# Output bias added by an accumulating DMA, half of the last sums on POOL, waits and router steps rearranged in a cross-attention and routed-FFN kernel

## The reference

```
def layernorm(x): return (x - mean(x)) / sqrt(var(x) + 1e-5)      # over the 256 features

q = layernorm(x) @ Wq + bq                # x, ctx: (128, 128, 256)
k, v = split(ctx @ Wkv + bkv)             # 16 heads of 16 each
scores = q @ k.T / 4
attn = softmax(scores, axis=2)            # over the QUERIES, not the keys
x1 = x + (attn @ v) @ Wo + bo

s = layernorm(x1) @ w_router              # one score for each token
top = the 96 of 128 tokens with the highest s, in each batch
h = layernorm(x1)
out = x1 + (gelu_tanh(h @ w_block) where in top, h elsewhere)
```

## Time and profile before

| | |
|---|---|
| median of 3 runs | 938.55 us (938.32 to 939.42) |
| the profiled execution | 938.16 us, of which the span from first to last instruction is 936.2 us |
| mean granted TensorE clock | 0.988 of 2.4 GHz |
| PE / PEld busy | 896.5 us (96%) / 758.3 us (81%) |
| DVE busy | 880.6 us (94%) |
| ACT busy | 875.5 us (94%) |
| POOL busy | 798.4 us (85%) |
| DMA | 70.84 MB, 25.6% of 16 engines on SP's queue |

### The profile page before, as it was taken

How to read it: one execution, slowest core, us unless ns; L and a number is a source line. 1 busy time by engine, 2 the same in 40 slices (tenths; PEclk the granted TensorE clock), 3 DMA queues, 4 the chain that set the end, 5 groups by cost and what they waited for, 6 DMA issues and landing times. The chain is left out here.

```text
span 936.2 us, 32893 instructions
## 1 busy us (share of the span) xinstructions
PE 896.5 (96%) x10296; PEld 758.3 (81%) x10296; DVE 880.6 (94%) x2318; ACT 875.5 (94%) x4499; POOL 798.4 (85%) x1488
## 2 busy tenths in 40 slices
PE   6899999999999999999999999999999999999972
PEld 5688888888888888888888888888888888888861
DVE  4898999999999999999999999999999999999877
ACT  2899999999999999999999999999999999999983
POOL 4367789999999999999999989999999999998865
PEclk8999999999999999999999999999999999999997
DMA  6222222232232232232223123223223223211102
GB/s 186 74 52 59 64 69 56 82 92 55 85 91 59 83 89 72 72 87 73 73 85 92 55 85 92 57 82 92 59 83 91 58 85 88 79 54 54 47 25 91
DMA packets 71244, 70.84 MB, mean 76 GB/s; under 512 B 12192, under 2 KB 62880, under 8 KB 71072
## 3 DMA queue, kind: packets, MB, share of 16 engines
q1 hardware_dynamic: 71072, 68.73, 25.6%
HBM read 35.13 MB, written 16.78 MB: 55 GB/s over the span
## 5 line engine op out<-in xcount | busy, mean ns | idle before, releaser
L532 ACT ACTIVATE e_sb<-ps_s,neg_max 128x128 f32<-128x128 f32 x2048 | 717.2, 411 | 8.3 <-DVE neg_max L644 8.2
L532 ACT ACTIVATION_READ_ACCUMULATOR e_sb<-ps_s,neg_max 128x1 f32 x2048 | 515.4, 252 | 0.0
L644 DVE TENSOR_REDUCE neg_max<-ps_s 128x4 f32<-128x512 f32 x512 | 330.5, 667 | 35.7 <-PE ps_s L324 35.2
L324 PE MATMUL ps_s<-q_eo,k_sb 32*128 32x256 f32 x2048 | 147.6, 401 | 9.7 <-DMA q_eo<-q_raw 3.6
L377 PE MATMUL ps_a<-e_sb,v_pad 128*32 128x128 f32 x4096 | 138.4, 276 | 2.1 <-POOL v_pad L969 0.7
L294 PE MATMUL ps_a<-w_o_sb,o_sb 128*128 128x256 f32 x512 | 135.7, 387 | 2.3 <-DVE v_sb L736 2.0
L969 POOL TENSOR_TENSOR v_pad<-v_sb,recip 128x256 f32<-128x256 f32 x128 | 79.4, 620 | 67.8 <-DVE recip L688 62.5
L294 PE MATMUL ps_t<-w_z_sb,xt_sb 128*128 128x258 f32 x512 | 132.7, 381 | 1.4 <-DVE z_sb L747 1.4
L324 PEld LDWEIGHTS ps_s<-q_eo,k_sb 32*128 32x128 f32 x2048 | 95.6, 185 | 39.0 <-issue 33.4
L377 PEld LDWEIGHTS ps_a<-e_sb,v_pad 128*32 128x32 f32 x4096 | 104.1, 109 | 24.0 <-issue 21.7
L959 POOL TENSOR_TENSOR x_sb<-x_sb,bo_sb 128x256 f32<-128x256 f32 x128 | 119.0, 931 | 0.2
(11 more groups left out here) (92 smaller groups left out, 2199.2 us busy)
## 6 DMA issues: line engine op xcount, KB each, us to landing
x_sb<-in_x SPq DMA_DIRECT2D x64, 256.0 KB, 2.9
c_sb<-in_ctx SPq DMA_DIRECT2D x64, 256.0 KB, 3.1
q_eo<-q_raw SPq DMA_DIRECT2D x512, 32.0 KB, 2.0
out<-z_sb SPq DMA_DIRECT2D x64, 256.0 KB, 2.4
...
```

What stands on the lines that cost most here:

```text
L324: mm = nc.tensor.matmul(ps_s[:, bank(b, j), c, :, :], k_sb[rows, r2, c, h * T:(h + 1) * T], q_eo[rows, r2, :, c, h, :], start=True, stop=True)
L532: last = nc.scalar.activation(e_sb[:, b % 4, j, c, par, :], ps_s[:, bank(b, j), c, par, :], ACT.Exp, bias=neg_max[:, b % 4, h:h + 1], accu ...
L644: nc.vector.tensor_reduce(neg_max[:, b % 4, :].rearrange("p (c j q) -> p j c q", c=C, j=J)[:, j, :, :], ps_s[:, bank(b, j), :, :, :], AX.X ...
```

## The change

Four things are changed together.

1. The output bias is no longer added to x by a POOL instruction for each batch. POOL issues one DMA for four batches that adds bo_sb to x_sb while it writes (`inputs_and_bias`); the residual waits for its landing (`xb_in`). 32 DMAs take the place of 128 instructions.
2. For the odd batches from 5 to 111 (54 of 128) the last sum is made by POOL in two instructions, `final_scaled` and `final_sum`, in place of one on DVE.
3. Waits: in the steps from 20 on, waits for work that other waits already cover are left out (parameter `settled`). On PE the waits ahead of the scores, the input transposes and attention are moved to earlier places: `pair_ready` and `inputs_ready` behind the projection, `scaled_values_ready` behind the block product, `router_bank_free` behind the transposes of x1.
4. DVE's order: `values_and_bias` stands ahead of `inputs_low`, and the router's eleven operations are spread over five steps in another way.

The diff, cut to its core. In the functions left out only the parameter `settled` and its `if` are added, as in `residual` below.

```diff
--- before
+++ after
...
@@ -199,6 +200,11 @@
 
         def u_on_act(b):
             return sum(1 for n in U_ON_ACT if n <= b)
+
+        FINAL_ON_POOL = tuple(range(5, B - 16, 2))
+
+        def finals_on_pool(b):
+            return sum(1 for n in FINAL_ON_POOL if n <= b)
...
 
                 if b % 2 == 0 and has(b):
-                    sp.wait_ge(final_ready, upto(b + 1))
+                    sp.wait_ge(final_ready, upto(b + 1) - finals_on_pool(b + 1))
+                    if b + 1 in FINAL_ON_POOL:
+                        sp.wait_ge(final_pool_ready, finals_on_pool(b + 1))
...
 
+            def pair_ready(b, settled=False):
+
+                if b % 2 == 0 and has(b):
+                    pe.wait_ge(q_eo_in[(b // 2) % 2], (b // 4 + 1) * 128)
+                    if not settled:
+                        pe.wait_ge(k_ready, upto(b + 1))
+
+            def inputs_ready(b):
+
+                if has(b):
+                    pe.wait_ge(xhat_ready, upto(b))
+                    if b % 2 == 0:
+                        pe.wait_ge(c_in[pair(b)], landed(b))
+
             def scores(b):
 
                 if not has(b):
                     return
                 r2, h = (b // 2) % 2, b % 2
-                if h == 0:
-                    pe.wait_ge(q_eo_in[r2], (b // 4 + 1) * 128)
-                    pe.wait_ge(k_ready, upto(b + 1))
+                if b == 0:
+                    pair_ready(b)
                 if has(b - 1):
-                    pe.wait_ge(exp_ready[3], upto(b - 1))
                     pe.wait_ge(exp_ready[1], upto(b - 1))
-                    pe.wait_ge(exp_ready[2], upto(b - 1))
-                if has(b - 2):
-                    pe.wait_ge(exp_ready[0], upto(b - 2))
-                if b % GROUP == 5 and has(b - 13):
-                    pe.wait_ge(cand_ready, upto(b - 13 + 7))
-                if b % GROUP == 1 and has(b - 17):
-                    pe.wait_ge(keep_col_ready, upto(b - 17 + 7))
                 for c in range(C):
                     for j in range(J):
                         rows = slice(32 * j, 32 * j + 32)
...
+                if b % GROUP == 5 and has(b - 13):
+                    pe.wait_ge(cand_ready, upto(b - 13 + 7))
+                if b % GROUP == 1 and has(b - 17):
+                    pe.wait_ge(keep_col_ready, upto(b - 17 + 7))
+
+            def transpose_inputs(b, settled=False):
 
                 if not has(b):
                     return
-                pe.wait_ge(xhat_ready, upto(b))
-                if b % 2 == 0:
-                    pe.wait_ge(c_in[pair(b)], landed(b))
+                if not settled:
+                    inputs_ready(b)
                 if has(b - 10):
                     pe.wait_ge(z_ready, upto(b - 10))
                 elif b == 2:
...
-            def attention(b):
+            def scaled_values_ready(b):
+
+                pe.wait_ge(v_pad_ready, upto(b))
+
+            def attention(b, settled=False):
 
                 if not has(b):
                     return
-                pe.wait_ge(v_pad_ready, upto(b))
+                if not settled:
+                    scaled_values_ready(b)
...
+                sure = 20 <= s < B - 8
                 scores(s)
-                transpose_inputs(s + 5)
+                transpose_inputs(s + 5, s > 2)
                 values(s - 1)
-                queries_or_keys(s + 2, 1)
-                queries_or_keys(s + 3, 0)
+                queries_or_keys(s + 2, 1, sure)
+                queries_or_keys(s + 3, 0, sure)
                 keep_columns(s - 16)
                 candidates(s - 12)
-                projection(s - 2)
-                block_product(s - 4)
-                transpose_x1(s - 3)
-                attention(s - 1)
+                projection(s - 2, sure)
+                pair_ready(s + 1, sure)
+                inputs_ready(s + 6)
+                block_product(s - 4, sure)
+                if sure:
+                    scaled_values_ready(s - 1)
+                transpose_x1(s - 3, sure)
+                router_bank_free(s + 1)
+                attention(s - 1, sure)
...
 
                 if has(b):
                     dve.wait_ge(o_mm, upto(b))
-                    dve.wait_ge(xb_ready, upto(b))
+                    if not settled or b % 4 == 0:
+                        dve.wait_ge(xb_in[b // 4 % 4], landed(b))
                     nc.vector.tensor_tensor(x1_sb[:, b % R, :], ps_proj, x_sb[:, b % R, :],
...
+
+                if has(b) and b not in FINAL_ON_POOL:
                     if b in U_ON_ACT:
                         dve.wait_ge(u_act_ready, u_on_act(b))
                     else:
...
 
             for s in range(2, B):
-                x1_transposed(s - 4)
+                sure = 20 <= s < B - 1
+                x1_transposed(s - 4, sure)
                 if s >= 4:
                     stats1(s + 10)
                 aggregate2(s - 3)
+                router(s - 13, 2)
+                router(s - 14, 4)
                 router(s - 15, 6)
+                router(s - 16, 8)
                 if s >= 4:
                     aggregate1(s + 10)
                 maxima(s, 3)
                 maxima(s, 2)
+                router(s - 16, 9)
+                values_and_bias(s - 1, sure)
                 inputs_low(s + 5)
-                values_and_bias(s - 1)
                 inverse_sums(s - 1)
                 maxima(s, 1)
-                queries(s + 3)
+                queries(s + 3, sure)
                 router(s - 16, 10)
-                router(s - 14, 5)
-                router(s - 15, 7)
-                router(s - 13, 2)
                 router(s - 12, 0)
-                keys(s + 2)
-                residual(s - 2)
+                keys(s + 2, sure)
+                residual(s - 2, sure)
                 maxima(s, 0)
                 if s == B - 1:
                     values_and_bias(B - 1)
                 router(s - 12, 1)
                 router(s - 13, 3)
-                final(s - 16)
+                router(s - 14, 5)
+                router(s - 15, 7)
+                final(s - 16, sure)
                 stats2(s - 2)
-                router(s - 15, 8)
-                product_scaled(s - 4)
-                router(s - 13, 4)
-                router(s - 15, 9)
+                product_scaled(s - 4, sure)
                 if s < 4:
...
 
-            def input_and_bias(b):
-
-                if has(b):
-                    pool.wait_ge(xhat_ready, upto(b))
+            def inputs_and_bias(b):
+
+                if b % 4 == 0 and has(b):
+                    pool.wait_ge(xhat_ready, upto(b + 3))
                     if b == 0:
                         pool.wait_ge(vo_bias_in, 32)
-                    nc.gpsimd.tensor_tensor(x_sb[:, b % R, :], x_sb[:, b % R, :], bo_sb[:, :],
-                                            ALU.add).then_inc(xb_ready, 1)
-
-            def values_over_sums(b):
+                    nc.gpsimd.dma_start(x_sb[:, b % R:b % R + 4, :],
+                                        bo_sb[:, :].rearrange("p (a e) -> p a e", a=1).to_broadcast([P, 4, E]),
+                                        accum_op=ALU.add).then_inc(xb_in[b // 4 % 4], 16)
+
+            def final_scaled(b):
+
+                if b in FINAL_ON_POOL:
+                    g, k, r = (b // GROUP) % 2, b % GROUP, b % R
+                    nc.gpsimd.tensor_scalar(z_sb[:, r, 0:E], z_sb[:, r, 0:E], half_keep[:, g, k:k + 1], None,
+                                            ALU.mult).then_inc(scaled_ready, 1)
+
+            def final_sum(b):
+
+                if b in FINAL_ON_POOL:
+                    pool.wait_ge(u_ready, upto(b))
+                    pool.wait_ge(scaled_ready, finals_on_pool(b))
+                    nc.gpsimd.tensor_tensor(z_sb[:, b % R, 0:E], z_sb[:, b % R, 0:E], x1_sb[:, b % R, :],
+                                            ALU.add).then_inc(final_pool_ready, 1)
...
+                sure = 20 <= s < B - 1
+                normalise(s + 7, sure)
                 rstd1_of_pair(s + 9)
                 rstd2_of_pair(s - 4)
-                gelu_square(s - 5)
-                values_over_sums(s - 1)
+                gelu_square(s - 5, sure)
+                values_over_sums(s - 1, sure)
+                inputs_and_bias(s + 4)
                 scale_and_shift(s - 16)
-                unprocessed(s - 16)
+                unprocessed(s - 16, sure)
                 gelu_factor(s - 5)
+                final_scaled(s - 16)
                 gelu_sum(s - 7)
-                input_and_bias(s + 4)
                 gelu_cubic(s - 5)
+                final_sum(s - 16)
                 gelu_product(s - 7)
 
             rstd2_of_pair(B - 4)
...
```

107 lines of the change are left out of this document (58 added, 49 removed).

## The result

The kernel after takes 942.26 us (median of 7 runs, 941.62 to 942.79), the kernel before, beside it, 939.02 us (7 runs, 938.32 to 939.55). The ratio is 1.0036, 95% interval 1.0024 to 1.0048: slower by 0.36%, 3.2 us on the medians, where the prediction had 925.3 us. The profiled execution's span is 941.0 us, before 936.2.

A forecast was written before the change was run, and what follows sets the result against it. PE was taken as the bound, its own step 6.78 us. Savings of 13.0 us over 104 steps, with the ends 14.2, less 1.3 for thin margin: 938.16 - 14.2 + 1.3 = 925.3 us, range 922.5 to 928.

The forecast's parts named there:

- D: Time one bias DMA holds POOL, taken as 1.0 us; POOL's 6.28 us plus D/4 had to fit a 6.81 us step.
- The rival on the slow side: POOL becomes the bound, deciding from D = 2.64 us; at D = 3.0, 949 us; chance 0.12.
- The values' bias: On DVE, v_sb would start 2.46 us after the scores instead of 3.06, ready before PE's projection.
- late values: PE's projection waits for the values with their bias: 0.61 us in eight steps, all to be saved.
- keep row to projection: On PE, a router transpose ahead of the projection adds 0.15 us in eight steps.
- the relief by the DMA: POOL loses its 0.97 us bias addition per step; POOL's resulting 6.53 us of 6.81 was counted as worth nothing.
- The waits: Ahead of even batches' scores on PE, fewer waits save 0.13 us in three steps of eight, 0.38 us.
- The idles of the weight load: On PE, 0.33 us before transposes and 0.20 before odd scores, put down to tiling mode changes, would stay.
- the rival that PE's own step shrinks: If idles before mode changes were waits, the loop over ACT bounds at 6.65 us: 910 us, chance 0.04.
- The last sums on POOL: DVE 0.39 us shorter every second step; worth nothing alone, but cover for the router's spreading, otherwise 0.3 us delay.

The follow-up runs named there:

- e1: The changed kernel with one line moved: POOL's bias DMA stands behind the mix (unprocessed), not ahead of it; 928.05 us, ratio 0.9878.
- e9: The kernel before with only the bias by DMA, issued behind the mix; order, waits and last sums as before; 936.76 us, ratio 0.9975.
- e4: The kernel before with only the bias by DMA, at the change's place ahead of the mix; 946.88 us, ratio 1.0088.
- e8: e7 plus two POOL multiplications into an unused tile ahead of the mix in every fourth step, DMA still behind it; 943.90 us, ratio 1.0046.
- e7: The changed kernel with the DMA moved behind the mix and all last sums on DVE again; 927.64 us, ratio 0.9872.
- e12: e7 with the keep row's 8-row transpose replaced by a matmul over a 128-row tile whose other rows are zero; 925.15 us, ratio 0.9847.
- e5: The kernel before with only DVE's new order (values' bias early, router spread); 937.90 us, ratio 0.9977.
- e3: The changed kernel with both POOL edits undone (no bias DMA, all last sums on DVE), leaving order and waits; 930.15 us, ratio 0.9899.
- e6: The kernel before with only the change's waits (taken out, and PE's moved); 931.70 us, ratio 0.9918.
- e2: The changed kernel with all last sums on DVE again, the DMA still ahead of the mix; 940.56 us, ratio 1.0015.

## Why the prediction was wrong

**The step that failed** is "Up to D = 4 x (6.81 - 6.28) = 2.1 us it stays hidden". D was mis-sized only a little, 1.37 us for 1.0, and POOL's throughput did hide it, as e1 shows, though with far less room than was claimed. By the prediction's own count POOL has 6.76 us of work a step in e1 (54.69 / 8, less 0.08 idle ahead of v_pad), not 6.53: the last sums came to (0.93 + 0.64) / 2 = 0.79 us a step for 0.63, the DMA to 0.34 for 0.25. With that, 4 x (6.81 - 6.44) = 1.5 us of D could be hidden, not 2.1. That did not yet bind. What failed is that the sum asked only how much work POOL has in a step, not who waits for the instructions behind the DMA. Three were looked at: v_pad, the landing, the store. The mix stands directly behind the DMA, `final` waits for it in the same step, and z, the transposes, the cast and the exps follow. e1 moves nothing but the DMA past the mix and gets 14.2 us back; e9 against e4 gets 10.1 us in the kernel before; e8 puts the same time there without a DMA and loses 16 us. The two DMAs of eight steps do not cost alike: that of batch 72, whose step also has two small operations ahead of the mix, lengthens the step behind it by 0.56 us in the change and 0.67 in e4, that of batch 76 by 0.23 and by nothing. Which of the router's operations makes the first so much dearer was not tried. The slack of that place can be bounded: 1.4 us ahead of the mix made DVE stand still for 1.01 us in the step shown and PE for 0.39 us, so the mix had some 0.4 us to spare for DVE and about 1 us for PE, an estimate for the step of batch 72 alone. The order in POOL's fence of the change showed the DMA ahead of the mix; the row that was missing from the argument was the one that says when the mix ends and the final starts.

**The rival on the slow side** had the right engine and the wrong mechanism: it wanted D over 2.64 us and all of POOL as the bound. The slowdown came with half of that, by latency behind the DMAs. The DMA row is 1.34 to 1.39 us in every kernel that adds four batches at a time, so nothing lengthened it there.

**The values' bias.** It starts 2.50 us after the scores, as told. But of the 0.61 us put on late values not all was theirs. The steps of batches 77 and 78 fall from 6.95 and 7.02 us before to 6.79 and 6.77 in e7, so 0.41 us were. The step with the keep row keeps its 0.21 us ahead of the transpose of 8 rows and its longer projection in e7, where the values are early; e12 shows 0.09 us of it to be the small tile's. The prediction had counted 0.15 us there (keep row to projection) and overlooked the interval in front of it and the longer projection behind it, together the other 0.2. And the order is worth 1.5 us by itself (e5) and 1.6 us beside the waits (930.15 against 931.70, in different sets and with overlapping intervals; 0.22 us in eight steps), while 8 us stood for it in the prediction. The cause was only in part the router's place on DVE. In e3, with order and waits, the step of batch 78 still takes 6.92 us; with the bias by DMA as well (e7) it takes 6.77, and DVE's last sum in the step of batch 76 is no longer 0.35 us longer by POOL's addition. The prediction put the relief by the DMA at nothing; it is worth 0.14 us in eight steps there (54.84 to 54.70) and 0.16 by itself (e9). What holds e5's 0.45 us was not tried.

**The waits** were right in mechanism and nearly in size: 0.43 us in eight steps for 0.38, 7.7 us on the medians for 5 (e6).

**The idles of the weight load** ahead of the transposes and the odd scores stayed at 0.33 and 0.20 us wherever nothing else was waited for, as the prediction had chosen. No step of the stretch is under 6.77 us in any kernel, so the rival that PE's own step shrinks falls.

**The last sums on POOL** were held to be the cover without which the router's spread would delay the exps. e7 has the spread without the cover, and its eight steps are as long as those of e1 (54.70 and 54.69 us). The cover was needless, and cost 1.7 us beside the DMA's delay (e2). Their multiplication took 0.93 us where 0.56 was taken.

**Sum.** With the DMA behind the mix the change gives 928.05 us, 0.9878: the forecast's 925.3 was 2.8 us too low even so. Eight steps take 54.69 us there (e1) where the forecast had 54.60, in an execution of 926.30 us, so 1.75 of the 2.8 us are the distance of e1's median from its profiled execution. With the keep row's tile out of the way (e12) they take 54.60 and the kernel 925.15 us.
